# Attention layer of a graph network: node sums in one PSUM bank, formed last in TensorE's turn; number row, phases and rounded angles moved to the bank that this leaves

## The reference

```python
rel_t_enc = jnp.cos(rel_t[:, None] * time_w[None, :] + time_b)      # E x 32
edge_attr = jnp.concatenate([rel_t_enc, msg], axis=-1)              # E x 96
q = q_all[dst]; k = k_all[src]; v = v_all[src]                      # 2 heads of 64
e = edge_attr @ We
alpha = jnp.sum(q * (k + e), axis=-1) / math.sqrt(CH)
m = segment_max(alpha, dst); ex = jnp.exp(alpha - m[dst])
denom = segment_sum(ex, dst)
out = segment_sum((v + e) * (ex / denom[dst])[:, :, None], dst)
out = out + x @ Wskip + bskip
```

## Time and profile before

| | |
|---|---|
| median of 3 runs | 9850.37 us (9843.33 to 9854.15) |
| the profiled execution | 9864.48 us, its span 9862.8 us |
| first layer's loop | about 430 to 5100 us |
| second layer and the two closings | about 5100 to 9862 us |
| busy share of the span | PE 77%, DVE 87%, ACT 52%, POOL 68% |
| PE's granted clock, mean | 0.82 of full speed |

### The profile page before, as it was taken

How to read it: one execution, slowest core, us unless ns; L and a number is a source line. 1 busy time by engine, 2 the same in 40 slices (tenths; PEclk the granted TensorE clock), 3 DMA queues, 4 the chain that set the end, 5 groups by cost and what they waited for, 6 DMA issues and landing times.

```text
span 9862.8 us, 272152 instructions
## 1 busy us (share of the span) xinstructions
PE 7624.6 (77%) x52868; PEld 7101.3 (72%) x52869; DVE 8560.3 (87%) x21301; ACT 5115.0 (52%) x20838; POOL 6708.6 (68%) x6871
## 2 busy tenths in 40 slices
PE   6477777777777777777756777788888888888855
PEld 2477777777777777777756777787888877877754
DVE  5899999999999999999987666799999999999968
ACT  2377777777777777777753333333333333333300
POOL 0477777777777777777745777777777777777720
PEclk8688988888888888898875555688888888888888
DMA  6467666676666666666632222355555555555544
GB/s 191 114 180 178 179 177 177 178 179 178 176 177 180 177 176 177 178 181 177 177 97 69 71 71 71 106 151 147 149 147 149 148 148 149 148 148 149 148 133 116
DMA packets 1631706, 1484.67 MB, mean 151 GB/s; under 512 B 792007, under 2 KB 1363043, under 8 KB 1631203
## 3 DMA queue, kind: packets, MB, share of 16 engines
q1 hardware_dynamic: 1374244, 848.34, 34.3%
q0 software_dynamic: 257088, 632.95, 22.8%
HBM read 1225.51 MB, written 254.87 MB: 150 GB/s over the span
## 4 chain that ended last, share of the span: by engine, by line
issue 25%; DVE 19%; POOL 18%; PE 14%; DMA 7%; ACT 7%; DVEq 6%; SPq 3%; ACTq 2%; POOLq 0%
POOL message_scratch L869 17%; DMA message_scratch<-ohT,idx 6%; PE bank L982 3%; DVE y_all L1537 3%; PE bank L973 3%; ACT arena L1154 2%; DVEq L531 2%; PE bank L955 2%; PE bank L1015 2%; PE bank L963 2%; DVE acc L1670 1%; SPq L728 1%; DVE oh L1583 1%; DVE oh L1576 1%; DVE kve L1523 1%
## 5 line engine op out<-in xcount | busy, mean ns | idle before, releaser
L817 POOL DMA_INDIRECT kv<-kv_scratch,arena x3136 | 3265.7, 1041 | 1236.6 <-issue 837.5
L869 POOL DMA_INDIRECT message_scratch<-ohT,idx x3232 | 3214.2, 994 | 1079.0 <-issue 880.2
L1261 ACT ACTIVATE ohT<-bank,kv 128x128 f32<-128x128 f32 x3232 | 923.9, 369 | 2703.8 <-DMA message_scratch<-ohT,idx 2665.1
L1154 ACT ACTIVATE arena<-arena,weights 128x65 f32<-128x65 f32 x7040 | 1771.6, 337 | 2.4 <-PE bank L982 2.3
L1063 PE MATMUL bank<-acc,oh 128*128 x6464 | 1211.2, 345 | 520.3 <-ACT ohT L1262 514.4
L1063 PEld LDWEIGHTS bank<-acc,oh 128*128 128x128 f32 x6464 | 1054.7, 247 | 627.7 <-issue 625.2
L1077 PE MATMUL bank<-oh,kve 128*128 128x128 f32 x8640 | 1387.7, 321 | 144.7 <-DVE arena L1838 107.8
L982 PE MATMUL bank<-arena,oh 128*128 128x130 f32 x7040 | 1164.1, 318 | 280.8 <-DVE acc L1670 274.8
L1077 PEld LDWEIGHTS bank<-oh,kve 128*128 128x128 f32 x8640 | 1248.0, 227 | 167.8 <-issue 157.3
L982 PEld LDWEIGHTS bank<-arena,oh 128*128 128x128 f32 x7040 | 1048.2, 227 | 362.6 <-issue 295.1
L973 PE MATMUL bank<-arena,ohT 128*128 128x128 f32 x7040 | 1090.6, 306 | 0.0
(11 more groups left out here) (232 smaller groups left out, 12653.6 us busy)
## 6 DMA issues: line engine op xcount, KB each, us to landing
kve<-message_scratch SPq DMA_DIRECT2D x2160, 129.0 KB
kve<-nodes_scratch SPq DMA_DIRECT2D x880, 256.0 KB
feat<-in_edge_attr_dram SPq DMA_DIRECT2D x880, 96.0 KB
feat<-block_scratch SPq DMA_DIRECT2D x812, 98.0 KB
arena<-q_scratch SPq DMA_DIRECT2D x880, 64.0 KB
message_scratch<-ohT,idx POOLq DMA_INDIRECT x3232
kv<-kv_scratch,arena POOLq DMA_INDIRECT x3136
feat<-in_edge_attr_dram SPq DMA_DIRECT2D x880, 32.0 KB
```

Of the source, the lines that this page charges most:

```text
L817: pool.indirect_dma_start(kv[:, k, g, :], None, kv_d, bass.IndirectOffsetOnAxis(ap=group_rows[:, half, k * G + g, 0:1].bitcast(I32), axis= ...
L869: pool.indirect_dma_start(msg_d, bass.IndirectOffsetOnAxis(ap=idx[:, k, g:g + 1], axis=0), sum_ring[:, k % RING1, g, :], None).then_inc(s_ ...
L1154: op = act.activation(wv[:, st.k % 2, g, h, :], vR[:, st.k, g, h, :], ACT.Copy, scale=weights[:, st.k // ROUND, g, st.k % ROUND, h:h + 1])
L1261: act.activation(sum_ring[:, st.k % RING1, g, 0:C], banks[2 + st.k % 2][:, g * P:(g + 1) * P], ACT.Copy, scale=taken[:, st.k, g, 2:3])
```

## The change

The node sums of even and odd steps no longer have a bank each: both lie in bank 6, side by side. PE's node sums of step s therefore wait until DVE has added the sums of step s - 1 (`wait(pe, s_acc, st.s)`), where they waited for step s - 2. In PE's turn they stand last, behind the edge term and the small matmuls, where they stood behind the features. Bank 7 is now DVE's own: it holds a copy of the number row, a copy of the phase offsets and the rounded angles (`turns`), which all lay in SBUF. Two copies ahead of the loop fill it.

```diff
-        turns = room(BATCH * G * TD).rearrange("p (b t) -> p b t", t=TD)
...
-        agg_ps = [banks[6 + j][:, 0:HEADS * HB] for j in range(2)]
+        agg_ps = [banks[6][:, j * HEADS * HB:(j + 1) * HEADS * HB] for j in range(2)]
         irow_ps, one_ps = banks[7][:, 0:P], banks[7][0:NB, P:P + 1]
+        brow_ps = banks[7][:, P:P + TD]
+        turns = banks[7][:, 2 * P:2 * P + BATCH * G * TD].rearrange("p (b t) -> p b t", t=TD)
...
                 pe.wait_ge(s_oh, st.s + 1)
-                wait(pe, s_acc, st.before(2))
+                wait(pe, s_acc, st.s)
...
-                    at(i, k, (feat_stage, 15), (sum_stage, 1), (q_stage, 14), (e_stage, 15))
+                    at(i, k, (feat_stage, 15), (q_stage, 14), (e_stage, 15))
                     if first_of(k, 5, ROUND):
                         at(i, k, (small_stage, 5))
                     if first_of(k, 4, ROUND):
                         at(i, k, (newT_stage, 4))
+                    at(i, k, (sum_stage, 1))
...
+            dve.tensor_copy(irow_ps, irow[:, :])
+            dve.tensor_copy(brow_ps, brow[:, :]).then_inc(s_tab, 1)
+            dve.wait_ge(s_tab, 3)
...
-                        op = dve.tensor_tensor(a, a, brow[:, :].unsqueeze(1).to_broadcast([P, BATCH * G, TD]), ALU.add)
+                        op = dve.tensor_tensor(a, a, brow_ps.unsqueeze(1).to_broadcast([P, BATCH * G, TD]), ALU.add)
...
-                dve.tensor_tensor(oh[:, st.k % QS, :, :], irow[:, :].unsqueeze(1).to_broadcast([P, G, P]),
+                dve.tensor_tensor(oh[:, st.k % QS, :, :], irow_ps.unsqueeze(1).to_broadcast([P, G, P]),
```

## The result

The changed kernel takes 10235.19 us (median of 4 runs, 10213.49 to 10268.75) against 9851.22 us before: ratio 1.0393, 95% interval 1.0372 to 1.0415. The prediction was 10274 us, and slower at 0.93. The profiled execution took 10213.5 us with a span of 10211.8, 349 us over the one before. The first layer's loop accounts for all of it: DVE's last node sums of the loop end at 5457 us, before at 5099.

What follows compares the result with a forecast made beforehand. DVE, busy 92% of the first layer's loop, was taken as the bound. Waits 2.35 + rounding output 0.5 + half clock 1.0 = 3.85 us a round, over 110 rounds 423 us, gave 10274 us; 8-in-10 range 10060 to 10460.

Steps and rivals of the forecast that it cites:

- The new wait and its chain: From DVE's end of turn through node sums, features, ACT's copy, weighing and phases to DVE: 5.1 us; waits 2.35 us a round.
- Turn 1 to 2: DVE's first angle instruction in turn 2 waits for ACT's phases: 0.8 us a round lost.
- Turn 3: DVE's scan waits for PE's transposes of the scores, which stand behind the node sums: 0.6 us a round.
- the clock term: PE falls to half clock in turns 1 and 3 after longer pauses: 1.0 us a round, bounds 0 and 2.3.
- Turn 5 to 6: Node sums ahead of the features delay phases by 1.74 us, less 0.90 of edge-term wait covered: 0.85 us a round.
- The operands: Rounding instruction slows by 124 ns with output in PSUM, four times a round: 0.5 us; other moved operands priced at nothing.
- The lower bound: Rounding instruction loses nothing if only the reading side counts, as its output is what moves: 0 us a round.
- the relief: POOL's gathers shorten as DVE reads fewer SBUF tensors, but POOL waits the gain away; alone 9846 us, chance 0.04.
- The faster rival: q and edge term behind the features alone, ending DVE's wait for the edge term: 9751 us, chance 0.04.
- Half clock throughout: PE at half clock in all the new chains, 2.3 us a round instead of 1.0: 10417 us, chance 0.20.

Runs made afterwards that it cites:

- e3: Kernel before with two banks and its old wait; only PE's order is new, node sums last in the turn: 9962.37 us, ratio 1.0126.
- e8: Kernel before with two banks and operands in SBUF, but with the new wait and the new order: 10190.57 us, ratio 1.0342.
- e10: Changed kernel with ACT's phases first in its turn, ahead of feature copy and weighings: 9876.02 us, ratio 1.0039.
- e9: Changed kernel with the scores transposed at the end of turn 2, ahead of the node sums: 10144.75 us, ratio 1.03.
- e1: Changed kernel with number row, phase offsets and rounded angles back in SBUF: 10180.67 us, ratio 1.0342.
- e5: Changed kernel, but PE forms the sums of step k, not k + 1, in turn k behind the features; ACT weighs one step later: 9898.35 us, ratio 1.0054.
- e6: Changed kernel with step k's sums in turn k behind the features, ACT weighing one step later, rounded angles in SBUF: 9849.67 us, ratio 1.0009.
- e4: Kernel before with two banks and its old wait; node sums moved behind the edge term, ahead of the small matmuls: 9706.98 us, ratio 0.9858.
- e12: Changed kernel with scores transposed ahead of the node sums and phases first in ACT's turn: 9690.68 us, ratio 0.9844.
- e2: Changed kernel with the rounded angles alone back in SBUF: 10155.16 us, ratio 1.0321.

## Why the prediction was right

*The new wait and its chain* were right: 5.16 us in the round shown against 5.1 forecast, and at the places named. The forecast that the node sums wait in nearly all turns went too far: they wait in 363 of 526, in none of turn 5, where they stand behind the maxima's transposes, and in about half of turns 2 and 6. e3 and e8 differ in the wait alone, 9962 against 10191; e10 and e9 take away the two ends of the chain one at a time.

*Turn 1 to 2*: 0.8 us plus a share of half clock. Turn 2 grew by 1.35, of which 0.12 is the rounding instruction: 1.23, so 0.43 from elsewhere. *Turn 3*: 0.6 plus a share of the clock; it grew by 1.16, 0.56 more. Together 0.99 us, where the clock term allowed 1.0 for both. That it meets the 1.0 so closely is luck: the prediction had bounds of 0 and 2.3 for it and no row to choose by.

The terms themselves can be read when the rounds are sorted by PE's clock records (worked out over the turns of the table). Where turn 1 had less than a fifth of its time at half clock (30 of 70 rounds), turn 2 took 5.86 us against 5.02 before: 0.84, and 0.72 without the rounding instruction. Where turn 3 had less than a fifth (20 rounds), it took 6.63 against 5.98: 0.65. These are the 0.8 and 0.6 of the sum. With turn 1 nearly all at half clock (12 rounds) turn 2 took 7.20.

That half clock reached turn 3 can also be read from the mean of L993, the transposes of the scores, 359 ns where L992 took 273:

```profile
L993 PE MATMUL bank<-ident,alpha 128*16 128x128 f32 x260 | 56.4, 359 | 0.0
```

```profile
L992 PE MATMUL bank<-ident,alpha 128*16 128x128 f32 x280 | 42.2, 273 | 117.2 <-DVE alpha L1544 117.2
```

*Turn 5 to 6* was the term that was mis-sized, for its mean: 0.85 forecast, 0.19 less 0.12 measured in the changed kernel, so 0.07. The step that failed is the one from a round with turn 5 at half clock, before and after, to the mean over all rounds. The mean granted clock of the loop hardly moved, 0.89 to 0.88: turns 1 and 3 took half clock, and turn 5, which was at half clock for 0.87 of its time before, was for 0.39 after (from the clock records, over the turns of the table). Sorted by that clock, turn 6 took 6.90 us before where turn 5 was nearly all at half clock (56 of 70 rounds), and 8.45 after (18 rounds): at the same clock it grew by 1.55, more than forecast. But in half of the rounds after (35) turn 5 had less than a fifth at half clock, and turn 6 took 6.32. So the longer queue costs what was forecast and more, and a turn 5 at full speed made up for it in the mean. The sum counted the clock as a pure addition. By the turn table this one term makes up 0.8 of the 0.86 us between the 3.85 us a round forecast and the 3.0 measured there. Alone, with the old wait (e3), the term is 0.81 by the turn table and 1.1 by the medians.

The range that the prediction gives with its chances, "10150 to 10370 by the bounds of its terms", doesn't come out of these terms: with the clock term at its bounds of 0 and 2.3 and the others as worked the sum is 10164 to 10417 us. The reading that nearly all of DVE's waits stand at turn 6 was from one round; over the table's turns it is four fifths.

*The operands* were right: 0.5 us a round forecast, 0.48 by the instruction's mean, 55 us by e1 and 49 by e5 and e6. The lower bound, that an output in PSUM might keep the doubled rate, is excluded: 417 ns for the same 256 columns. By the rule of the Trainium skill ("VectorE: DVE Perf Modes", section Why PSUM operands drop a tier) any PSUM operand ends the doubled mode of fp32 instructions; the trace agrees, 417 ns against 298, and here it is the output that lies in PSUM.

*The rivals.* POOL's gathers are shorter, 978 against 1041 ns, but not all of it is the operands: e1, with the chain and every operand in SBUF, has 1013. With the chain gone the relief is worth nothing (e6: 1002 ns, ratio 1.0009): DVE doesn't wait for POOL. The faster rival, with q and the edge term ahead of the sums, named a gain that exists: e4 has it. In the changed kernel it can't show, since the sums then hold up the features. Half clock throughout didn't come: turn 1 had it for 0.47 of its time and turn 3 for 0.39.

The medians differ by 384 us, the 3.0 us a round of the turn table over 110 rounds make 330. The rounds ahead of the table's grew more: the means over turns 8 to 160 are 42.7 us before and 46.8 changed, 4.1 more. In the profiled executions the whole loop is 357 us longer, 3.2 us a round, and what follows it 9 us shorter. From their 349 us to the 384 of the medians it is where the two executions lie among the runs: the one of the changed kernel 22 us under its median, the one before 13 over its.

**What stays open.** Why half clock left turn 5 when turns 1 and 3 took it. In e4 and e12 the granted clock is higher (0.92 and 0.93, against 0.89 before), so that PE's chains are shorter in many turns; whether the higher clock is a cause or a consequence of the shorter waits was not separated.

## What to carry to other kernels

In this kernel a wait moved by one step cost at most 0.2% in itself (e6); it cost by what stood behind the waiting instruction in its queue. Follow that queue through the next engine back to the bottleneck, add the durations, and compare with the shortest turn of the loop, not the mean one. And when a buffer's play is lost, reorder the followers first: moving two stages that nothing forced to stand behind the wait (phases, scores) turned a loss of 3.9% into a gain of 1.6%, and showed that the kernel before had the same fault in a milder form.

## What the runs showed of the hardware

Half clock moved between turns and its total hardly changed: PE's mean granted clock in the loop is 0.89 before, 0.88 changed, while turn 5 went from 0.87 to 0.39 of its time at half clock, turn 7 from 0.63 to 0.23, and turns 1 and 3 from nearly none to 0.47 and 0.39. A pause of about 2 us was not always followed by it. In the round shown, turns 1, 3 and 5 come behind pauses of PE of 2.25, 2.64 and 2.07 us; the first two were granted full speed, the third half (columns as in the earlier trace rows):

```profile
3020.50:3024.90 4.40, 3.55 (x29) 3.25 (x29) 4.23 (x9) 2.75 (x11) 3.22 (x4) 1.00 0.87 210
3030.90:3037.60 6.70, 5.18 (x43) 4.87 (x43) 6.14 (x11) 3.58 (x14) 5.03 (x6) 1.00 0.69 186
3043.50:3047.80 4.30, 4.30 (x21) 4.22 (x22) 3.97 (x10) 0.00 (x0) 1.91 (x2) 0.50 0.42 124
```

A DVE instruction with one input and an output of 128x256 takes 417 ns into PSUM and 298 to 313 into SBUF (before, e2, e1). Moving one of two SBUF inputs to PSUM left the comparison (679 to 678 ns) and the addition (422 to 417) as they were within 5 ns. POOL's gathers took 35 ns less with the operands in PSUM than with the same order and the operands in SBUF (978 in the changed kernel, 1013 in e1), and 40 less without the chain (1002 in e6, 1042 before); the chain alone took off 29.
